# An int8-style decoder layer on one core: an earlier gamma/beta load, one joint scale chain for weights and activations, context products inside the QKV maximum pass, and bf16 diagonals

## The chip, the cores and the metric

The kernel runs on one core of one Trainium2 chip. The metric is the device time of one execution in microseconds (us). The kernel before took 493.25 us (median of 3 runs, 491.62 to 495.28). The profiled execution took 491.34 us, of which the trace covers a span of 489.4 us; the remaining 1.9 us lie around the span.

The engines are PE (TensorE), PEld (its weight load), DVE (VectorE), ACT (ScalarE), POOL (GpSimd) and SP (SyncE, which here only issues DMAs).

## The reference, cut to what matters

```python
def fq_floor(x):                    # fq_round is the same with round
    s = 2 ** ceil(log2(max(|x|) / 127))          # one scale for the WHOLE tensor
    return clip(floor(x / s), -128, 127) * s

h    = layernorm(x) * fq_round(ln_gamma) + fq_round(ln_beta)     # x: 8 x 256 x 128
qkv  = fq_floor(fq_floor(h) @ fq_round(w_qkv))                   # w_qkv: 128 x 3072
dots = fq_floor(q @ k.T * temp)                                  # 16 heads of 64, temp from exp(log_temp)
attn = fq_floor(softmax(dots))
out  = fq_floor(fq_floor(attn @ v) @ fq_round(w_out))
x    = layernorm(x + out)
# cross attention without softmax: q, k, v of 16 heads of 8 from x and the context (8 x 512 x 128);
# kv = sum over t of k[t] v[t], att = q @ kv * scale; x = layernorm(att + x), layernorm again outside
# MLP with affine quantisation and an exact gelu; x = layernorm(x + mlp)
```

Each `fq_` needs the maximum of a whole tensor before one element of it can be rounded. So the kernel computes the QKV product twice: once for its maximum (the maximum pass) and once for its codes (the code pass). It does the same with the dots.

Because the cross attention has no softmax, its context side folds into one 128 x 128 matrix for each batch. From the Gram matrix of the context, `gram = ctx^T [ctx | 1]`, come `a1 = gram Wv^T + bias`, then `kv`, then the matrix `xm`. These are the "context products".

## The kernel before, in words

The program is written out by hand for each engine, with semaphores between them. Each engine runs its list in order. Its stages on the time axis of the trace are these.

- **Prologue** (0 to 42.7 us). SP and ACT issue the loads. DVE takes the maximum of gamma and beta. The maximum goes across the partitions in `across_send` (the identity times the value of each partition, a 128 x 128 fp32 diagonal), a PE product with a matrix of ones (`across`), and `across_take` (a reduce of the result). `scale_of` makes the power of two and its inverse with three tiny DVE instructions. Then come the layernorm of x in 16 tiles of 128 tokens (`bn_stats`, `bn_aggr`, a square root on ACT, a Newton step, 16 instructions `norm`), PE transposes, gamma and beta applied while leaving PSUM (`hT`), and the maxima of `w_qkv` and of `hT` with a chain for each. Last come the integer codes of both (`h_codes`, `w_piece`), and on DVE the rounding of the temperature. ACT cannot start the maximum pass before DVE gets behind these seven tiny instructions, since DVE raises `qkv_folded` there.
- **QKV maximum pass** (42.7 to 78.9 us). It has 48 units of 128 x 1024, two matmuls each, in a ring of 4 slots of two PSUM banks, which are all 8 banks. Of every 4 units ACT takes the absolute value of 3 into bf16 (L835), and DVE folds each of those into a running maximum (L1164). DVE reads the fourth itself from PSUM (`absmax`, L1013). The loops over the four groups are hardware loops.
- **Between the passes**: DVE folds three running maxima into one and sends it across. PE makes the row sums of the context, both halves of `a1`, and in their midst the product with the diagonal. Then follows the **QKV code pass** (90.0 to 133.8 us), 48 units in a ring of 3 slots; banks 6 and 7 hold the other context products.
- Then the dots maximum pass, the dots code pass with the exponentials, the product with v, the output projection, the layernorms, the cross attention and the MLP.

In the trace, L476 is every matmul, L496 and L501 the PE transposes of the prologue, L1009 and L1010 every `tensor_scalar` of DVE, L1013 every maximum of absolute values, L1032 the reduce after `across`, L854 the codes on ACT. `mem` is the large SBUF array of which nearly every tile is a part, and `fold` is the store of the diagonals.

## Time and profile before

| | us |
|---|---|
| median of 3 runs | 493.25 (491.62 to 495.28) |
| profiled execution | 491.34 |
| its span | 489.4 |
| busy: DVE / ACT / PE / POOL | 423.3 / 341.4 / 240.0 / 153.3 |

The page cuts the span into 40 slices of 12.2 us and gives the busy share of each engine in tenths, and the clock granted to PE in tenths of 2.4 GHz. In a view in order of time a row reads: start, duration, engine, line, operation, tiles, and in brackets how long the engine was idle before it and what released it. A row with x2 or x16 holds that many merged instructions. An fp32 matmul appears as two records.

### The profile page before, as it was taken

The numbers are of one execution on the slowest core, as the hardware profiler recorded it, in microseconds if no ns is written. First come the engines' busy times: TensorE is split into PE (matmuls) and PEld (weight loads), VectorE is DVE, ScalarE is ACT, GpSimd is POOL, SyncE is SP. The second block draws the span as 40 slices with busy tenths as digits, with TensorE's granted clock in tenths as the row PEclk, the third lists the DMA queues.
The fourth block names the chain that finished last, engine by engine and source line by source line (L and its number), as shares of the span: only waits on it lengthen the run. The fifth ranks groups of instructions, "written<-read, shape, count | busy, mean of one in ns | idle before, by whom it ended". The sixth has DMA issues, their size and how long they took to land.

```text
span 489.4 us, 7119 instructions
## 1 busy us (share of the span) xinstructions
PE 240.0 (49%) x1538; PEld 108.3 (22%) x1546; DVE 423.3 (86%) x1415; ACT 341.4 (70%) x765; POOL 153.3 (31%) x324
## 2 busy tenths in 40 slices
PE   0096667988667763122222222207999528305031
PEld 0081123433212211011111111102333425202021
DVE  0898997497989998999999999969896986987967
ACT  1018993588899991999999999983677735636233
POOL 4700000200100000688888888881000003530010
PEclk9998996699955555555555555557999775557557
DMA  8500000000044432288888888876000400000002
GB/s 275 128 0 1 0 0 0 1 23 21 22 186 177 172 129 109 66 190 184 184 187 188 187 188 187 188 150 140 2 1 1 146 1 1 0 1 1 0 0 86
DMA packets 84207, 43.13 MB, mean 88 GB/s; under 512 B 69063, under 2 KB 74455, under 8 KB 84058
## 3 DMA queue, kind: packets, MB, share of 16 engines
q1 hardware_dynamic: 82090, 42.16, 33.2%
q10 hardware_dynamic: 2096, 0.73, 0.7%
q8 instruction: 8, 0.13, 0.1%
q14 instruction: 13, 0.11, 0.1%
HBM read 7.75 MB, written 1.58 MB: 19 GB/s over the span
## 4 chain that ended last, share of the span: by engine, by line
DVE 55%; PE 26%; issue 10%; ACT 5%; DMA 2%; DVEq 1%; ACTq 0%
PE ps L476 25%; DVE mem L1258 12%; DVE d_max L1013 8%; DVE mem L1010 6%; DVE mem L1449 2%; DVE row_max L1258 2%; DMA gbc<-in_L_attn_ln_beta 2%; DVE m L1586 2%; DVE m L1587 2%; DVE mem L1164 2%; DVE neg_max L1009 1%; ACT mem L888 1%; DVE r_now L1009 1%; ACT mem L854 1%; DVE row_code L1009 1%
## 5 line engine op out<-in xcount | busy, mean ns | idle before, releaser
L476 PE MATMUL ps<-mem 64*128 64x256 bf16 (+5 forms) x1181 | 176.0, 356 | 133.5 <-DMA mem<-mem 81.3
L888 ACT ACTIVATE mem<-mem,neg_max 128x256 f32<-128x256 int16 x256 | 126.3, 494 | 13.6 <-DVE neg_max L1009 9.7
L476 PEld LDWEIGHTS ps<-mem 64*128 64x128 bf16 (+4 forms) x1188 | 71.3, 122 | 234.4 <-issue 146.1
L1258 DVE CUSTOM_DVE_ANT_0 mem<-ps,fold,c 128x256 int16<-128x256 f32 x256 | 111.3, 471 | 0.0
L434 POOL TENSOR_SCALAR mem<-mem,r_now 128x256 int16<-128x256 f32 x176 | 80.9, 478 | 81.4 <-DVE r_now L1009 81.4
L1164 DVE TENSOR_TENSOR mem<-mem 128x1024 bf16<-128x1024 bf16 x84 | 54.4, 690 | 3.5 <-ACT mem L835 3.5
L835 ACT ACTIVATE mem<-ps,c 128x1024 bf16<-128x1024 f32 x48 | 48.3, 1291 | 1.6 <-PE ps L476 1.6
L888 ACT ACTIVATION_READ_ACCUMULATOR mem<-mem,neg_max 128x1 f32 x256 | 47.7, 186 | 0.0
L854 ACT ACTIVATE mem<-ps,c 128x1024 int16<-128x1024 f32 x32 | 36.3, 1210 | 13.9 <-PE ps L476 13.8
L434 POOL TENSOR_SCALAR bv_fine<-mem,r_now 128x256 int16<-128x256 f32 x80 | 36.8, 478 | 5.0 <-DVE r_now L1009 5.0
L1013 DVE TENSOR_REDUCE d_max<-ps 128x1024 f32 (+1 forms) x34 | 38.0, 1127 | 0.0
L1010 DVE TENSOR_SCALAR mem<-mem,c 128x2048 bf16<-128x2048 int16 (+2 forms) x44 | 34.7, 811 | 3.6 <-PE ps L476 3.4
L835 ACT ACTIVATE mem<-ps 128x1024 bf16<-128x1024 f32 x36 | 34.2, 1031 | 2.6 <-DVEq L1144 1.9
L476 PE MATMUL ps<-fold,ones 128*128 128x128 f32 (+2 forms) x18 | 7.3, 499 | 50.6 <-DVE fold L1009 50.6
L446 POOL TENSOR_TENSOR mem<-mem 128x512 f32<-128x512 f32 x4 | 5.0, 1267 | 77.3 <-ACT mem L945 77.3
L902 ACT ACTIVATE mem<-ps 128x1024 bf16<-128x1024 f32 x15 | 15.4, 1025 | 19.3 <-PE ps L476 19.3
L476 PE MATMUL ps<-minus,mem 128*128 128x256 bf16 x128 | 25.8, 285 | 2.5 <-DVE mem L1010 2.5
L1010 DVE TENSOR_SCALAR mem<-ps,c 128x1024 int16<-128x1024 f32 (+1 forms) x17 | 21.8, 1283 | 1.0 <-PE ps L476 0.9
L409 POOL MEMSET mem<- 128x3072 bf16 x1 | 2.7, 2657 | 62.5 <-DVE c L1009 62.5
L1258 DVE DVE_READ_ACCUMULATOR2_ANT row_max<- 128x1 f32 x256 | 20.1, 78 | 0.0
L1215 DVE CAST mem<-mem 128x1024 bf16<-128x1024 int16 x32 | 12.4, 422 | 6.7 <-ACT mem L854 6.7
L905 ACT ACTIVATE mem<-ps 128x1024 f32<-128x1024 f32 x16 | 16.4, 1022 | 2.5 <-DVE d_max L1013 2.5
(202 smaller groups left out, 371.5 us busy)
## 6 DMA issues: line engine op xcount, KB each, us to landing
mem<-mem SPq DMA_DIRECT2D x64, 256.0 KB, 2.4
mem<-in_L_attn_w_qkv SPq DMA_DIRECT2D x1, 1536.0 KB, 9.4
mem<-in_x SPq DMA_DIRECT2D x1, 1024.0 KB, 5.5
out<-mem SPq DMA_DIRECT2D x4, 256.0 KB, 2.2
mem<-in_x ACTq DMA_DIRECT2D x1, 512.0 KB, 5.5
mem<-in_x SPq DMA_DIRECT2D x1, 512.0 KB, 4.8
xattn_matrix<-mem SPq DMA_DIRECT2D x1, 512.0 KB
mem<-in_L_attn_w_out SPq DMA_DIRECT2D x1, 512.0 KB, 5.0
```

Source lines behind the costliest of these rows:

```text
L434: ins = pl.tensor_scalar(fine_ring[slot][:, u, pos * N:(pos + 1) * N], e_ring[:, unit % 4, pos], r_now[:, unit % 4, pos:pos + 1], FLOOR, A ...
L476: return te.matmul(o_, l_, r_, start=start, stop=stop)
L835: sc.activation(abs_t[:, k % 3], ps[:, s:s + 2].rearrange("p a n -> p (a n)"), ACT.Abs, scale=scale).then_inc(sem(f"{phase}_max_act"), 1)
L854: sc.activation(code_i[:, k % 4], ps[:, s:s + 2].rearrange("p a n -> p (a n)"), ACT.Identity, scale=col("g_qkv"), bias=col("floor")).then_ ...
L888: ins = sc.activation(e_ring[:, u % 4, pos], y_ring[:, u % 4, pos], ACT.Exp, scale=scale_reg, bias=neg_max[:, u % 4, pos:pos + 1], accum_o ...
L902: sc.activation(abs_o[nth % 4], src, ACT.Abs, scale=GROW).then_inc(sem("o_abs"), 1)
L905: sc.activation(o_pair(nth // 4, nth % 4), src, ACT.Copy).then_inc(sem("o_read"), 1)
L1009: return ve.tensor_scalar(o_, i_, s1, None, op0)
L1010: return ve.tensor_scalar(o_, i_, s1, s2, op0, op1)
L1013: return ve.tensor_reduce(o_, i_, AX.X, ALU.max, apply_absolute_value=True)
L1164: ve.tensor_tensor(run_max[:, k % 3], run_max[:, k % 3], abs_t[:, k % 3], ALU.max)\
L1258: ins = ve.tensor_tensor_reduce(y_ring[:, slot, pos], ps[:, 2 * slot + pos // 2, (pos % 2) * N:(pos % 2 + 1) * N], shift, col("g_dots"), - ...
```

## The change

- **Loads.** Both halves of x are issued by SP, in front of `w_qkv` and the context. ACT's queue begins with gamma and beta; the second half of x no longer stands ahead of them.
- **Prologue on DVE.** The statistics of the first eight tiles of x stand between sending and taking gamma's and beta's maximum. Half of the 16 `norm` go to ACT, which gets a shift `nmr0` for them. Both halves of `hT` are made on ACT. The maxima of `w_qkv` and `hT` go through one chain (`wh_scale`). The growth factor is in the diagonal instead of an instruction of its own. The temperature is computed behind the scale of QKV.
- **POOL.** The two products that spread the biases (`bv_sel`, `bk_sel`) become 16 ACT instructions on 8 partitions ahead of the square root. The temperature's chain on POOL comes before the memset of `run_max`, which now waits for gamma's codes.
- **Maximum pass.** It is written out without loops and has a ring of 3 slots. Banks 6 and 7 hold the context products, which PE does between units: half of a batch's Gram matrix after each of the units 6 to 21, the sums after 27, `a1` after 28, 31, 32 and 34. ACT takes them out after units 13, 20, 24, 28 and 37. DVE's last fold is done after the others have been joined (in both maximum passes).
- **After it.** PE makes the first three units of the code pass before the product with the diagonal. That product is bf16 for QKV, dots and the attention output (`across_bf`).

```diff
@@ sync, pool @@
-            sp.dma_start(x_in_pairs[:, halves[0]], x_pairs[:, halves[0]]).then_inc(sem("x_first"), 16)
+            for half in range(2):
+                batches = slice(half * B // 2, (half + 1) * B // 2)
+                sp.dma_start(x_in_pairs[:, batches], x_pairs[:, batches]).then_inc(sem(f"x_half{half}"), 16)
...
-            pl.memset(run_max, 0.0).then_inc(sem("run_max_zero"), 1)
-
-            eye = ident[0:B, 0:B].rearrange("p (b o) -> p b o", o=1).to_broadcast((B, B, D))
-            pool.wait_ge(sem("bkv_loaded"), 32)
-            pl.tensor_tensor(bv_sel, bkv[:, 1:2].to_broadcast((B, B, D)), eye, ALU.mult)
-            pl.tensor_tensor(bk_sel[:], bkv[:, 0:1].to_broadcast((B, B, D)), eye, ALU.mult)\
-                .then_inc(sem("bias_rows"), 1)
...
+            pool.wait_ge(sem("gb_codes"), 1)
+            pl.memset(run_max, 0.0).then_inc(sem("run_max_zero"), 1)
@@ tensor @@
+            def across_bf(bank):
+
+                n_across[0] += 1
+                pe.wait_ge(sem("diagonals"), n_across[0])
+                mm(ps[:, bank, 0:P], ones_bf[:], diag_b[:, 0]).then_inc(sem("across"), 1)
...
+            def gram_half(b, part):
+                bank, pos = (6, 7, 6)[b // 3], b % 3
+                for k in range(2 * part, 2 * part + 2):
                     last = mm(ps[:, bank, pos * (D + 1):(pos + 1) * (D + 1)], ctx_sb[:, 4 * b + k, 0:D],
                               ctx_sb[:, 4 * b + k], k == 0, k == 3)
...
+            def ctx_work(n):
...
+                if n == 18:
+                    pe.wait_ge(sem("gram_ready"), 1)
+                if 6 <= n < 22:
+                    gram_half((n - 6) // 2, n % 2)
+                if n == 27:
+                    pe.wait_ge(sem("gram_ready"), 3)
+                    pe.wait_ge(sem("bias_rows"), 1)
+                    sums_of_ctx()
+                if n == 28:
+                    a1_main(0)
+                if n == 31:
+                    pe.wait_ge(sem("cs_r2"), 1)
+                    a1_bias(0)
+                if n == 32:
+                    a1_main(1)
+                if n == 34:
+                    a1_bias(1)
...
-            with pe.Fori(0, GROUPS) as gi:
+            for gi in range(GROUPS):
                 for u in range(QKV_UNITS):
...
                     qkv_unit(gi, u, u % QKV_MAX_RING).then_inc(sem("qkv_max_unit"), 1)
...
+                    ctx_work(gi * QKV_UNITS + u)
...
-            a1_half(0)
             pe.sem_inc(sem("dots_max_unit"), 2 * STAGES)
-
-            across(5, diag, 1)
-            a1_half(1)
...
                     qkv_unit(gi, u, u % QKV_RING).then_inc(sem("qkv_code_unit"), 1)
+                    if n == QKV_RING - 1:
+                        across_bf(7)
@@ scalar @@
-            act.dma_start(x_in.rearrange("p (b c) d -> p b (c d)", c=2)[:, B // 2:B],
-                          x.rearrange("b (p c) d -> p b (c d)", c=2)[:, B // 2:B]).then_inc(sem("x_second"), 16)
             act.dma_start(gbc[:, 0:1], at_g[:, None]).then_inc(sem("gb_loaded"), 16)
...
+            for b in range(B):
+                sc.activation(bv_sel[:, b], bkv[:, 1], ACT.Copy, scale=ident[0:B, b:b + 1])
+                ins = sc.activation(bk_sel[:, b], bkv[:, 0], ACT.Copy, scale=ident[0:B, b:b + 1])
+            ins.then_inc(sem("bias_rows"), 1)
             sqrt_of("ln0")
+            act.wait_ge(sem("ln0_shift"), 1)
...
+                for part, at_n, bank, b0, nb in ((0, 13, 6, 0, 3), (1, 20, 7, 3, 3), (2, 24, 6, 6, 2)):
+                    if n == at_n:
                         act.wait_ge(sem("gram_ps"), part + 1)
@@ vector @@
+            def across_bf(bank):
+
+                ts(diag_b[:, 0], ident_b[:], col("m"), None, ALU.mult).then_inc(sem("diagonals"), 1)
+                across_take(1, bank, col("x"))
...
-            link(ts(x6[:, 0:2], x6[:, 0:2], GROW, None, ALU.mult))
             scale_of(x6[:, 0:2], 2, s4[:, 0:2], i4[:, 0:2])
...
+            across(m6[:, 2:4], 2, diag6[:, 2:4], 7, x6[:, 2:4], 2)
+            scale_of(x6[:, 2:4], 2, s4[:, 2:4], i4[:, 2:4], done="wh_scale")
```

The first place is DVE's list from the maximum of gamma and beta on. Before:

```order
L1013 TENSOR_REDUCE m<-gbc 128x2
L1009 TENSOR_SCALAR mem<-ident,m 128x128 x2
L1032 TENSOR_REDUCE x<-ps 128x2
L1009 TENSOR_SCALAR x<-x 128x2
L1010 TENSOR_SCALAR s<-x 128x2
L1009 TENSOR_SCALAR s<-s 128x2
L1010 TENSOR_SCALAR i<-s 128x2
L1009 TENSOR_SCALAR gb_i<-gbc,i 128x1 x2
L1009 TENSOR_SCALAR c<-gb_i,s 128x1 x2
L1067 BN_STATS mem<-mem 128x6 x16
```

And now, with what each row waits for:

```order
L1058 TENSOR_REDUCE m<-gbc 128x2 [waits gb_loaded,consts]
L1055 TENSOR_SCALAR mem<-ident,m 128x128 [waits dve_chain]
L1113 BN_STATS mem<-mem 128x6 [waits x_half0]
L1113 BN_STATS mem<-mem 128x6 x7
L1082 TENSOR_REDUCE x<-ps 128x2 [waits across]
L1055 TENSOR_SCALAR s<-x 128x2 [waits dve_chain]
L1054 TENSOR_SCALAR s<-s 128x2 [waits dve_chain]
L1055 TENSOR_SCALAR i<-s 128x2 [waits dve_chain]
```

Eight statistics moved into the wait for PE, and the row `x<-x 128x2` is gone.

The second place is PE between the passes. Before:

```order
L566 MATMUL ps<-ident,mem 8x128 [waits qkv_max_dve,qkv_max_act,bias_rows]
L476 MATMUL ps<-xw_T,mem 8x128
L476 MATMUL ps<-bkv,s 8x128
L476 MATMUL ps<-xw_T,mem 128x128 x4
L476 MATMUL ps<-bv_fine,cs_T 128x512 [waits cs_T]
L476 MATMUL ps<-fold,ones 128x128 [waits diagonals]
L476 MATMUL ps<-bv_fine,cs_T 128x512
L476 MATMUL ps<-mem 128x512 [waits qkv_code_act]
```

And now:

```order
L475 MATMUL ps<-mem 128x512 [waits qkv_max_act]
L475 MATMUL ps<-mem 128x512 [waits qkv_max_dve]
L475 MATMUL ps<-mem 128x512
L475 MATMUL ps<-diag_b,ones_bf 128x128 [waits diagonals]
L475 MATMUL ps<-mem 128x512 [waits qkv_code_act]
```

Only units of the code pass stand ahead of the product with the diagonal; the context products are further up, between units of the maximum pass.

## Rows read from the trace of the kernel before

**Rows 1.** The page, part 2: busy tenths and granted clock in 40 slices

```profile
DVE  0898997497989998999999999969896986987967
...
PEclk9998996699955555555555555557999775557557
```

**Rows 2.** DMA issues of the first 30 us: KB, us from issue to landing

```profile
mem<-in_x SPq DMA_DIRECT2D x1, 512.0 KB, 4.8
```

**Rows 3.** In order of time, 0 to 26 us

```profile
3.46 0.30 POOL L376 TENSOR_SCALAR ident_b<-ident 128x128 bf16<-128x128 f32 x1
...
11.88 0.15 DVE L1013 TENSOR_REDUCE m<-gbc 128x2 f32<-128x2 f32 x1 [11.88 <-DMA gbc<-in_L_attn_ln_beta]
...
13.93 0.42 DVE L1032 TENSOR_REDUCE x<-ps 128x2 f32<-128x256 f32 x1 [1.38 <-PE ps L476]
14.27 1.89 POOL L384 TENSOR_TENSOR bk_sel<-bkv,ident 8x1024 f32<-8x1024 f32 x1
14.39 1.79 DVE L1009 TENSOR_SCALAR x<-x 128x2 f32<-128x2 f32 x1
...
17.17 0.19 POOL L389 TENSOR_SCALAR c<-lt 128x1 f32<-128x1 f32 x1 [1.02 <-DMA lt<-in_L_attn_log_temp]
...
21.87 0.31 ACT L800 ACTIVATE sd<-mem,c 128x16 f32<-128x16 f32 x1 [13.82 <-DVE mem L1071]
...
23.82 0.19 POOL L405 TENSOR_TENSOR c<-c 128x1 f32<-128x1 f32 x1
```

**Rows 4.** In order of time, 25 to 46 us

```profile
27.62 1.34 DVE L1010 TENSOR_SCALAR mem<-ps,c 128x1024 f32<-128x1024 f32 x1
...
29.75 3.74 PE L476 MATMUL ps<-mem 128*128 128x129 f32 x32
...
35.28 0.28 DVE L1032 TENSOR_REDUCE x<-ps 128x1 f32<-128x128 f32 x1
...
36.42 0.28 DVE L1032 TENSOR_REDUCE c<-ps 128x1 f32<-128x128 f32 x1
...
40.83 0.43 DVE L1117 CAST mem<-mem 128x1024 bf16<-128x1024 int16 x1
...
42.67 3.77 ACT L835 ACTIVATE mem<-ps 128x1024 bf16<-128x1024 f32 x4 [1.88 <-DVEq L1144]
```

**Rows 5.** DVE's groups by shape, 0 to 136 us: count, busy us, mean ns, idle before

```profile
L1010 DVE TENSOR_SCALAR mem<-mem,rsd 128x128 f32<-128x128 f32 x16 | 4.2, 342 | 0.0
```

**Rows 6.** One group of 12 units of the maximum pass as a window: busy of PE, PEld, DVE, ACT, POOL; clock

```profile
48.30:57.10 8.80, 6.11 (x23) 1.77 (x24) 8.80 (x14) 8.62 (x10) 0.00 (x0) 1.00 0.00 0
```

**Rows 7.** ACT's groups by shape, 0 to 190 us

```profile
L858 ACT ACTIVATE mem<-ps 128x1024 f32<-128x1024 f32 x1 | 1.0, 1022 | 0.0
L819 ACT ACTIVATE mem<-ps 128x387 f32<-128x387 f32 x2 | 0.9, 478 | 0.0
...
L843 ACT ACTIVATE cs_T<-ps 8x128 f32<-8x128 f32 x1 | 0.3, 266 | 1.9 <-PE ps L566 1.9
```

**Rows 8.** In order of time, 74 to 112 us

```profile
80.48 2.08 PE L476 MATMUL ps<-xw_T,mem 128*128 128x128 f32 x8
82.48 2.07 PE L476 MATMUL ps<-bv_fine,cs_T 8*128 8x512 f32 x2
...
84.48 0.80 PE L476 MATMUL ps<-fold,ones 128*128 128x128 f32 x2
...
85.32 0.29 DVE L1032 TENSOR_REDUCE c<-ps 128x1 f32<-128x128 f32 x1 [2.18 <-PE ps L476]
...
86.54 2.66 POOL L409 MEMSET mem<- 128x3072 bf16 x1 [62.53 <-DVE c L1009]
...
89.32 4.11 PE L476 MATMUL ps<-mem 128*128 128x512 bf16 x9 [0.33 <-issue]
...
91.28 0.43 DVE L1215 CAST mem<-mem 128x1024 bf16<-128x1024 int16 x1 [4.49 <-ACT mem L854]
...
97.80 1.02 PE L476 MATMUL ps<-mem,xw_T 128*128 128x512 f32 x2
```

More of the change, by code:

```diff
@@ L491, in _ @@
             across(7, diag6, 2)
-            for half in range(2):
-                pe.wait_ge(sem("xn_ready"), half + 1)
-                for t in range(8 * half, 8 * half + 8):
+            for q in range(4):
+                pe.wait_ge(sem("xn_ready"), q + 1)
+                pe.wait_ge(sem("xn_act"), q + 1)
+                for t in range(4 * q, 4 * q + 4):
                     last = te.transpose(ps[:, t // 4, (t % 4) * P:(t % 4 + 1) * P], xn[:, t], ident[:])
-                last.then_inc(sem("xnT_ps"), 1)
+                if q % 2:
+                    last.then_inc(sem("xnT_ps"), 1)
             pe.wait_ge(sem("xw_loaded"), 48)
@@ L589, in kv_bias @@
                 for b in range(4 * half, 4 * half + 4):
-                    last = mm(ps[:, 6 + half, (b % 4) * P:(b % 4 + 1) * P], bk_sel[:, b], r2[:, 0],
+                    last = mm(ps[:, 6 + half, (b % 4) * P:(b % 4 + 1) * P], bk_sel[:, b], r2,
                               False, b % 4 == 3)
@@ L1081, in _ @@
             link(ve.tensor_tensor(rsd[:], rsd[:], newton[:], ALU.mult))
-            for t in range(TILES):
-                ins = norm(xn, x_in, t)
-                if t % 8 == 7:
-                    ins.then_inc(sem("xn_ready"), 1)
-            dve.wait_ge(sem("gb_codes"), 1)
-            dve.wait_ge(sem("xnT_ps"), 1)
-            ts(hT[:, 0:UNIT], ps[:, 0:2].rearrange("p a n -> p (a n)"), col("gamma"), col("beta"),
-               ALU.mult, ALU.add).then_inc(sem("hT_ready"), 1)
-            dve.wait_ge(sem("w_loaded"), 16)
@@ L1150, in max_pass @@
                     order.insert(u - EARLY, u)
-                with dve.Fori(0, iters) as i:
+                for i in range(iters):
                     for u in order:
@@ L1166, in max_pass @@
[L1166 to L1177 removed]
+                            continue
```

280 lines of the change are left out of this document (147 added, 133 removed).

## The prediction

> **What bounds the kernel now.** I read the page's slices first, then the prologue in order of time with its DMA issues, then one group of the maximum pass as a window, then the rows between the passes.
>
> The slices [rows 1] show DVE at nine tenths almost everywhere and at nothing in the first slice. So what shortens DVE's own list, or the time before that list begins, comes off the end. The second line shows PE's clock high (2.4 GHz) through slice 5, that is to 73 us, low (1.2 GHz) for a good part of slices 6 and 7, around the end of the maximum pass, and high again in the code pass. The change touches four places.
>
> - **The start.** DVE's first instruction comes at 11.88, released by beta's landing [rows 3]. The first half of x, at the head of SP's queue, landed 4.8 after its issue, near 5.6 [rows 2]. The constants were ready at 3.76 [rows 3]. The order of loads costs DVE some 7 us.
> - **The prologue** is one chain on DVE from 11.88 to ACT's first row of the maximum pass at 42.67, which was idle for 1.88 until DVE raised a semaphore [rows 4].
> - **The maximum pass.** In 8.80 us DVE is busy 8.80, ACT 8.62 and PE 6.11 [rows 6]. Two engines are full, and the third has 2.7 us to spare for every 12 units, 0.733 us for each unit.
> - **Between the passes** DVE waits 2.18 for PE and 4.49 for ACT [rows 8], while PE makes context products at the low clock.
>
> **The change, part by part.**
>
> *Loads, -6.9.* Beta would now be issued near 1.4, with no half of x ahead on its queue. Its landing isn't in the trace. The floor is 3.8, where the constants are ready; the ceiling is 11.9, if nothing improves. The nearest row is x's first half, at 5.6, with a thousand times the bytes. I take 5.0: 11.9 - 5.0 = 6.9.
>
> *DVE's chain to the first maximum unit, -7.4.*
> - PE's first product: DVE waited 1.38 [rows 3]. Eight statistics fill that: -1.4.
> - The growth instruction `x<-x`: -1.8 [rows 3], see below.
> - Eight of 16 `norm` go to ACT. Sixteen are busy 4.2 [rows 5]: -2.1.
> - The half of `hT` that DVE made: -1.3 [rows 4]. ACT makes it under DVE's maximum of `w_qkv`, which doesn't need it.
> - The temperature lies between the last cast, ending at 41.26, and 42.67 [rows 4]: -1.4. It comes back below.
> - The joint chain saves the stretch from one reduce to the other (35.28 to 36.42 [rows 4]), 1.1, but its double-width product makes DVE wait 1.38 as the first did, and the second diagonal and wider reduce add about 0.1: +0.4. The shift `nmr0` is another small instruction, +0.2 as an estimate.
>
> The 16 ACT copies that replace POOL's products take at most 0.27 each, 4.3 in all [rows 7]. They stand ahead of the square root. That came at 21.87, 10.0 after DVE's first instruction [rows 3]. Now it is due 10.0 - 1.4 - 1.8 = 6.8 after it, near 11.8. If the biases land by 7.5 the copies are hidden and cost nothing. If they land where they did (POOL's first product ended when its second began, at 14.27), the square root is late; that belongs to the first rival.
>
> *The memset of `run_max` and DVE, +1.3.* The 1.79 of `x<-x` at 14.39 end at 16.18. POOL's product with `bk_sel` ran from 14.27 to 16.16 [rows 3]. A DVE instruction of two elements per partition stood still until POOL had finished. The change removes this pair, but moves POOL's 2.66 memset [rows 8]. It used to run while DVE had nothing to do. Now it follows the temperature's chain on POOL, which ran from 17.17 to 24.01 [rows 3]; it may begin up to 3 us sooner, since the loads ahead of `lt` move up. So the memset lies somewhere from 21 to 27. By the sums above, DVE is then at the joint diagonals, the scale chain or the first codes, all SBUF to SBUF `tensor_scalar`. The old memset shows nothing, since DVE then had only one-element instructions. Bounds: 0 and 2.66; I take the middle, 1.3. The Trainium skill, page "SBUF — State Buffer", section "Who interferes with whom", speaks against the change here: a VectorE instruction in a two-port mode (`tensor_scalar` and casts can be) and any GpSimd instruction exclude each other for the whole instruction, writes included. The pair at 14.27 agrees with it. By that rule the term is near 2.7 instead of 1.3, and the sum 1.4 higher.
>
> *Context products in the maximum pass, +4.8.* A unit costs PE 6.11/12 = 0.51, perhaps 0.47 without gaps. Gram: 32 records in 3.74 [rows 4] are 16 matmuls, so a half of two matmuls is 0.47. Units 6 to 21 then cost PE 0.94 to 0.98 against a cadence of 0.733: 16 x 0.2 to 0.25 = 3.3 to 3.9 too much. A ring of three slots lets PE be about two units ahead at the start, worth 1.5: +2.2. The halves of `a1` took 2.08 and 2.07 at 1.2 GHz [rows 8]; at 2.4 GHz I take 1.04 and 1.02 (the 512-column product at 97.80 [rows 8]), twice 2.06, and 0.8 for the sums: 4.9 in units 27 to 34. Eight units leave PE 8 x 0.733 - 8 x 0.49 = 2.0. The remaining 2.9, less the same cushion, is +1.4. ACT's outputs of Gram (0.48 each [rows 7]) fall where PE is late anyway. That of `a1`, 1.02 [rows 7], falls behind it, where ACT is full: +1.0. The smaller ring adds perhaps 0.2. Bounds: +2.0, if PE keeps up and only ACT's outputs count; +7.8, with no cushion (3.9 + 2.9 + 1.0).
>
> *Between the passes, -5.1.* DVE's 2.18 for PE hold the `a1` product ahead of the diagonal and 0.80 of fp32 [rows 8]. One bf16 pass is one record instead of two: 0.4. With half of a diagonal's write, -1.9. The 4.49 for ACT's first code go, because three units stand ready. The temperature takes 1.3 of that place: -3.2. The fold's new order saves nothing: the same instructions still follow DVE's own last maximum.
>
> *Code pass, -1.0:* ACT's output of `a1` is gone. Bounds 0, if DVE is full regardless, and -2, with PE warm sooner.
>
> *The rest, -1.4:* bf16 diagonals for dots and output, 0.5 each as above; two growth instructions, 0.2 each as an estimate. Loops written out on DVE: nothing, the loop shows no gap at DVE 8.80 of 8.80.
>
> Sum: -6.9 - 7.4 + 1.3 + 4.8 - 5.1 - 1.0 - 1.4 = **-15.7**. The profiled execution of 491.34 becomes 475.6. The median shown is 1.9 higher, so I say **477.5**.
>
> **The rivals.**
>
> - *Beta or the biases stay late (12%).* For it: tiny loads took 9.9 where x took 4.8, and their packets share the DMA engines with x's. Against: they no longer follow half of x. The first term vanishes: 477.5 + 6.9 = 484.4.
> - *The full lock (13%).* The page's rule taken as a mechanism of this kernel: a diagonal or the first code of `hT` waits for the memset's end, 2.66. 478.9.
> - *The context products are free (12%).* PE's 2.7 spare per group times four is 10.8, and the products need 16 x 0.47 + 4.9 = 12.4; if matmuls overlap better than records show, only ACT's 2.0 stay: 474.7, and with the copies well hidden 473.
> - *Slower: PE falls to 1.2 GHz in the maximum pass (5%).* The clock fell near the end of the pass [rows 1] and stayed low from 80 to 89 although PE had fp32 products one after another: 0.80 for one across, 2.07 for 512 columns against 1.02 later [rows 8]. Now PE idles before the pass, then half of its work is fp32. At the low clock nine records of a unit take 4.11 [rows 8], 0.91 per unit, 44 for 48; Gram doubles to 15, the rest to 10: 69 against about 36 now, +33 in place of +4.8. That gives 505.7. It is slower than before as soon as about 60% of the pass runs low. Against: Gram ran at full speed after fp32 transposes [rows 4], and a bf16 unit now follows every piece.
>
> The forecast has 55%; 3% are left for what I don't see. Its own range is 472 to 482.5.
>
> **Range and chances.** Down: the pass at +2.0 (-2.8), no lock (-1.3), beta at 3.8 (-1.2), code pass -2 (-1.0), not all at once: 470.5. Up: the pass at +7.8 (+3.0), full lock (+1.4), copies partly open (+1.5) is 483.4; the late beta is 484.4, so 484.5. A measurement here tells about 1% from no change, 488.3 to 498.2. Only the clock case lies above it, 5%; 3% for within; 92% faster.
>
> **What would show it.** DVE's first row near 5 and statistics behind it; ACT's first row of the maximum pass near 29 to 30; that pass near 41 long, with DVE and ACT idle on PE in units 6 to 21 and 28 to 35; ACT's first code without a wait for PE; a DVE `tensor_scalar` that ends with the memset. Wrong if beta lands after 8, if the clock row shows 5 in slices 2 to 5, or if the pass lasts 36 or 46.

## The result and the profile after

The changed kernel takes **480.39 us** (median of 4 runs, 479.80 to 482.28), the kernel before beside it on the same chip 492.47. The ratio is 0.976, 95% interval 0.973 to 0.979. Its profiled execution took 479.80, with a span of 478.0, against 491.34 and 489.4 before. The forecast was 477.5, its range 470.5 to 484.5.

Since nearly every row moved, the two traces are compared at landmarks that both have. Times are from the start of the span; "pass" is the QKV maximum pass.

| stretch | before | after | difference | forecast |
|---|---|---|---|---|
| start to DVE's reduce of gamma and beta | 11.88 | 5.46 | -6.42 | -6.9 |
| to ACT's first absolute value of the pass | 30.79 | 25.20 | -5.59 | -6.1 (-7.4 and +1.3) |
| to the end of DVE's last maximum of the pass | 36.20 | 41.33 | +5.13 | +4.8 |
| to ACT's first code | 11.17 | 7.38 | -3.79 | -5.1 |
| DVE's first cast to the dots' first absolute value | 42.99 | 42.81 | -0.18 | -1.0 |
| all that follows, and what lies between these | | | -0.55 | -1.4 |
| span | 489.4 | 478.0 | -11.4 | -15.7 |

The page's slices of the changed kernel, DVE's busy tenths and PE's granted clock, answer to [rows 1]:

```profile
DVE  5879897889899999999999999958986985977967
...
PEclk9969995999755555555555555558999775557557
```

DVE works in the first slice. The clock is now low in parts of slices 2 and 6 (from 24 and from 72 us), in both of which PE had stopped. Before, it was low from 77.5 to 94.6 us, although PE was busy for 15.5 of the 17 us from 78 to 95. Both kernels thus open the code pass at the low clock, and that turns out to matter.

**The prologue**, in order of time, answers to [rows 3]:

```profile
5.46 0.15 DVE L1058 TENSOR_REDUCE m<-gbc 128x2 f32<-128x2 f32 x1 [5.46 <-DMA gbc<-in_L_attn_ln_beta]
...
8.68 0.40 ACT L823 ACTIVATE bv_fine<-bkv,ident 8x128 f32<-8x128 f32 x1 [0.71 <-DMA bkv<-in_L_xattn_bv]
...
13.36 0.29 ACT L816 ACTIVATE sd<-mem,c 128x16 f32<-128x16 f32 x1
13.69 0.25 DVE L1133 RECIPROCAL rsd<-sd 128x16 f32<-128x16 f32 x1 [1.49 <-ACT sd L816]
...
21.99 2.66 POOL L404 MEMSET mem<- 128x3072 bf16 x1
...
22.84 1.96 DVE L1055 TENSOR_SCALAR mem<-ident,m 128x128 f32<-128x128 f32 x2
24.85 1.22 PE L475 MATMUL ps<-mem,ones 128*128 128x256 f32 x2 [5.25 <-DVE mem L1055]
26.11 0.42 DVE L1082 TENSOR_REDUCE x<-ps 128x2 f32<-128x256 f32 x1 [1.31 <-PE ps L475]
```

Two things are to be seen. The square root stands at 13.36 directly behind the 16 copies, and DVE waits 1.49 for it: the copies are not hidden. And the two diagonals at 22.84, of a form that took 0.48 for two at 5.65, take 1.96 and end at 24.80, just behind the memset's end at 24.65.

**The pass.** PE in a window over units 6 to 21 (columns as in [rows 6]), and ACT's rows in the same stretch and at the output of `a1`:

```profile
36.00:47.70 11.70, 11.70 (x84) 9.66 (x83) 10.81 (x14) 9.48 (x12) 0.00 (x0) 1.00 0.01 2
```

```profile
36.92 2.85 ACT L873 ACTIVATE mem<-ps 128x1024 bf16<-128x1024 f32 x3 [0.65 <-PE ps L475]
...
40.42 1.94 ACT L873 ACTIVATE mem<-ps 128x1024 bf16<-128x1024 f32 x2 [0.65 <-PE ps L475]
...
63.41 1.03 ACT L860 ACTIVATE mem<-ps 128x1024 f32<-128x1024 f32 x1
```

PE is busy 11.70 of 11.70 where it was busy 6.11 of 8.80 [rows 6], and ACT waits for it once in every four units, which now take 3.50 (36.92 to 40.42) instead of 2.93. The granted clock is 1.00 there.

**Between the passes**, answering to [rows 8]:

```profile
76.28 0.29 PE L475 MATMUL ps<-diag_b,ones_bf 128*128 128x128 bf16 x1 [3.63 <-DVE diag_b L1054]
76.60 0.29 DVE L1082 TENSOR_REDUCE c<-ps 128x1 f32<-128x128 f32 x1 [0.38 <-PE ps L475]
...
79.37 4.63 ACT L903 ACTIVATE mem<-ps,c 128x1024 int16<-128x1024 f32 x4 [8.51 <-DVEq L1250]
80.61 0.43 DVE L1265 CAST mem<-mem 128x1024 bf16<-128x1024 int16 x1 [1.32 <-ACT mem L903]
...
84.66 1.28 DVE L1055 TENSOR_SCALAR mem<-ps,c 128x1024 int16<-128x1024 f32 x1 [1.29 <-PE ps L475]
...
85.09 1.20 ACT L903 ACTIVATE mem<-ps,c 128x1024 int16<-128x1024 f32 x1 [1.09 <-PE ps L475]
```

DVE waits 0.38 for PE instead of 2.18. But ACT's first code is released by DVE's sequencer: a semaphore that DVE raises behind the temperature. And 4 us into the code pass both engines wait for PE, at the low clock.

### The profile page after: what moved, and what is told of

It is laid out like the page before. It is cut to its first block, busy times and chain, and to the rows that moved or that the text cites. A ratio compares the mean times of both kernels' runs of the same rounds, so it can differ in the third digit from the quotient of the medians.

```text
span 478.0 us, 6808 instructions
## 1 busy us (share of the span) xinstructions
PE 233.2 (49%) x1541; PEld 106.5 (22%) x1541; DVE 420.0 (88%) x1396; ACT 350.2 (73%) x789; POOL 149.9 (31%) x323
## 4 chain that ended last, share of the span: by engine, by line
DVE 53%; PE 21%; issue 16%; ACT 7%; DMA 1%; DVEq 1%; ACTq 0%
PE ps L475 20%; DVE mem L1308 12%; DVE mem L1055 6%; DVE mem L1213 4%; DVE d_max L1058 4%; DVE mem L1496 2%; DVE row_max L1308 2%; DVE m L1633 2%; DVE m L1634 2%; ACT mem L903 2%; ACT mem L933 1%; DVE r_now L1054 1%; DMA bkv<-in_L_xattn_bv 1%; DVE row_code L1054 1%; DVE neg_max L1054 1%
## 5 line engine op out<-in xcount | busy, mean ns | idle before, releaser
L475 PEld LDWEIGHTS ps<-mem 64*128 64x128 bf16 (+3 forms) x1188 | 72.2, 122 | 229.0 <-issue 126.7
L1058 DVE TENSOR_REDUCE d_max<-ps 128x1 f32<-128x1024 f32 (+1 forms) x34 | 38.0, 1126 | 0.3 <-PE ps L475 0.3
L1055 DVE TENSOR_SCALAR mem<-mem,c 128x2048 bf16<-128x2048 int16 (+2 forms) x42 | 33.3, 814 | 3.8 <-PE ps L475 3.7
L475 PE MATMUL ps<-fold,ones 128*128 128x128 f32 (+2 forms) x10 | 4.6, 559 | 44.3 <-DVE fold L1055 44.3
L1055 DVE TENSOR_SCALAR mem<-ps,c 128x1024 int16<-128x1024 f32 x16 | 20.5, 1281 | 1.5 <-PE ps L475 1.5
L971 ACT ACTIVATE sd<-mem,c 128x4 f32<-128x4 f32 x16 | 4.6, 295 | 18.5 <-DVE mem L1503 18.3
```

The lines of the kernel that those rows point to most:

```text
L475: return te.matmul(o_, l_, r_, start=start, stop=stop)
L1055: return ve.tensor_scalar(o_, i_, s1, s2, op0, op1)
L1058: return ve.tensor_reduce(o_, i_, AX.X, ALU.max, apply_absolute_value=True)
```

## The experiments

All kernels are compared by the same landmarks, since gains of a microsecond drown in the total. "Beta" is DVE's first row, the others are the lengths of the stretches of the table above; beta, stretches and span come from one profiled execution. The last two columns are the ratio to the kernel before and its interval, over all executions.

| kernel | beta | to the pass | pass | to code | code pass | span | ratio | 95% |
|---|---|---|---|---|---|---|---|---|
| before | 11.88 | 30.79 | 36.20 | 11.17 | 42.99 | 489.4 | | |
| changed | 5.46 | 25.20 | 41.33 | 7.38 | 42.81 | 478.0 | 0.976 | 0.973-0.979 |
| changed, again | 7.46 | 23.77 | 41.32 | 7.37 | 42.79 | 478.5 | 0.977 | 0.974-0.980 |
| e1 temperature late | 7.76 | 23.52 | 41.32 | 6.18 | 43.91 | 478.7 | 0.974 | 0.971-0.977 |
| e2 copies late | 6.74 | 23.95 | 41.32 | 7.38 | 43.23 | 478.5 | 0.977 | 0.975-0.980 |
| e3 memset early | 7.44 | 22.46 | 41.32 | 7.38 | 43.95 | 478.6 | 0.973 | 0.970-0.976 |
| e4 half the Gram | 7.04 | 24.22 | 39.18 | 7.38 | 43.91 | 477.8 | 0.971 | 0.968-0.973 |
| e5 PE kept busy | 6.83 | 24.18 | 41.31 | 7.33 | 42.02 | 477.6 | 0.970 | 0.967-0.974 |
| e6 products respread | 7.16 | 25.09 | 37.70 | 7.45 | 44.25 | 477.8 | 0.970 | 0.967-0.974 |
| e7 a1 output late | 7.42 | 23.57 | 40.66 | 7.45 | 44.33 | 479.8 | 0.976 | 0.971-0.981 |
| o1 before, new loads | 7.33 | 31.17 | 36.19 | 11.17 | 43.11 | 485.3 | 0.987 | 0.984-0.990 |
| o2 before, ring of 3 | 11.98 | 32.34 | 36.48 | 10.14 | 42.59 | 490.5 | 1.000 | 0.998-1.002 |
| c1 all | 3.94 | 27.81 | 37.48 | 6.13 | 42.22 | 473.7 | 0.965 | 0.961-0.969 |
| c2 all, Gram split | 3.94 | 22.76 | 37.53 | 6.12 | 42.02 | 469.1 | 0.959 | 0.956-0.962 |

### The temperature behind the semaphore

```diff
-            temperature()
...
             dve.sem_inc(sem("cast_a"), 4)
+            temperature()
```

> Only the temperature's seven DVE instructions move, from ahead of the two semaphore increments that free ACT's code slots to behind them. Theory A (ACT's first code waits for those increments, not for the scale): ACT's first code comes 0.3 us after the scale instead of 1.7, and DVE's first cast about 1.3 us sooner against the scale; whole kernel 1.0 to 1.3 faster than the changed kernel (480.4), near 479.2. Theory B (the first code waits for PE or for the scale itself, the temperature is covered): the gap from scale to first code stays at 1.7 and the time at 480.4.

Measured: 479.94 us (479.28 to 480.76). ACT's first code comes 6.18 behind DVE's last maximum instead of 7.38:

```profile
78.78 2.30 ACT L903 ACTIVATE mem<-ps,c 128x1024 int16<-128x1024 f32 x2 [7.31 <-DVEq L1249]
```

The term is real, 1.20. But the code pass took 43.91 instead of 42.81, and 1.1 of the gain was gone in this execution. The move has a side effect too: DVE's first wide cast of the code pass now meets POOL's second memset and takes 1.36, where it took 0.43 at 80.61.

```profile
78.44 2.66 POOL L408 MEMSET mem<- 128x3072 bf16 x1 [53.18 <-DVE c L1054]
80.01 1.36 DVE L1265 CAST mem<-mem 128x1024 bf16<-128x1024 int16 x1
```

This is a rival for the lost 1.1, but the other runs speak against it. In e3 and e4 the cast takes 0.43 and the code pass is as long (43.95, 43.91). In c2 it takes 1.36 and the pass is 42.02, as in e5, where it takes 0.43.

### The copies behind xw_T

```diff
-            act.wait_ge(sem("bkv_loaded"), 32)
-            for b in range(B):
-                sc.activation(bv_sel[:, b], bkv[:, 1], ACT.Copy, scale=ident[0:B, b:b + 1])
-                ins = sc.activation(bk_sel[:, b], bkv[:, 0], ACT.Copy, scale=ident[0:B, b:b + 1])
-            ins.then_inc(sem("bias_rows"), 1)
             sqrt_of("ln0")
...
             sc.activation(xw_T[:].rearrange("p k n -> p (k n)"), ps[:, 6, 0:2 * P], ACT.Copy).then_inc(sem("xw_T"), 1)
+            act.wait_ge(sem("bkv_loaded"), 32)
...
```

> The 16 bias copies on ACT move from ahead of the first square root to behind the copy of the cross-attention weights, where ACT idles about 6 us. Theory A (the copies made the square root late): the square root starts near 12.1 instead of 13.36, DVE's wait of 1.49 for it goes down to about 0.3, and everything behind moves up by 1.2; near 479.2. Theory B (the square root is bound by DVE's statistics): the square root stays where it is. If the memset on POOL keeps its place in time while DVE's diagonals come 1.2 sooner, part of the gain shows up as a longer or shorter stall there: the diagonals would then meet the memset at its very start, so up to 1.2 may be lost again.

Measured: 481.28 us (480.29 to 481.33), no gain. DVE's wait for the square root is gone,

```profile
13.64 0.25 DVE L1133 RECIPROCAL rsd<-sd 128x16 f32<-128x16 f32 x1 [0.17 <-ACT sd L816]
```

but it comes at 13.64, where it came at 13.69. Beta had landed at 6.74 instead of 5.46. In the changed kernel's second profile (beta at 7.46, copies in front) the same row waits 0.17 as well. So DVE's chain and ACT's copies end nearly together at the square root: the copies cost 1.3 only when beta lands early. They take away what an early landing would give.

### The memset in front of the temperature's chain on POOL

```diff
+            pool.wait_ge(sem("gb_codes"), 1)
+            pl.memset(run_max, 0.0).then_inc(sem("run_max_zero"), 1)
             pool.wait_ge(sem("lt_loaded"), 16)
...
-            pool.wait_ge(sem("gb_codes"), 1)
-            pl.memset(run_max, 0.0).then_inc(sem("run_max_zero"), 1)
```

> POOL's memset of the running maxima moves ahead of the temperature's chain, so that it runs right after gamma's codes, from about 9.4 to 12.0, under DVE's statistics. Theory A (the memset held DVE's SBUF to SBUF tensor_scalar): the two diagonals at 22.8 take 0.48 together instead of 1.96, and all behind moves up by 1.5; near 478.9. DVE's bn_stats and bn_aggr are not slowed. Theory B (the long diagonal has another cause, such as the reduce before it): it stays at 1.96 and the time at 480.4.

Measured: 479.41 us (478.49 to 480.50). The diagonals take 0.48 again:

```profile
23.54 0.48 DVE L1055 TENSOR_SCALAR mem<-ident,m 128x128 f32<-128x128 f32 x2
24.07 0.50 PEld L475 LDWEIGHTS ps<-mem,ones 128*128 128x128 f32 x2 [3.85 <-DVE mem L1055]
24.07 1.22 PE L475 MATMUL ps<-mem,ones 128*128 128x256 f32 x2 [3.61 <-DVE mem L1055]
```

From beta to the pass it is 22.46, against 23.77 in the second profile of the changed kernel, which had beta at the same time: 1.3 for the lock. Again the code pass was longer, 43.95.

### Half of the Gram matrix left out

```diff
-                for k in range(2 * part, 2 * part + 2):
+                for k in range(2 * part, 2 * part + 1):
...
-                              ctx_sb[:, 4 * b + k], k == 0, k == 3)
+                              ctx_sb[:, 4 * b + k], k == 0, k == 2)
```

> Leaves out half of the Gram matmuls (one of the two in each piece), so the context products of units 6 to 21 cost PE 0.23 instead of 0.47 us each. Theory A (PE bounds units 6 to 21, 0.875 us for each where 0.735 would do): the pass falls from 41.3 us by 16 x 0.14 = 2.2 or a little more, to 39; near 478.1. Theory B (the ring of 3 slots sets the pace there, not PE's work): the pass stays above 40.5. Theory C (ACT's extra evictions alone lengthen the pass): it stays at 41.3.

Measured: 478.25 us (477.87 to 479.50). The pass is 39.18, 2.14 shorter, so PE's Gram work is the binding load in units 6 to 21. The code pass of the profiled execution gave back 1.1 for the third time.

### PE kept busy between the passes

```diff
                     if n == QKV_RING - 1:
+                        for k in range(16):
+                            mm(ps[:, 6, :], w5[:, 0, 0, 0], hT_codes[:, 0:BANK])
                         across_bf(7)
+                        for k in range(18):
+                            mm(ps[:, 6, :], w5[:, 0, 0, 0], hT_codes[:, 0:BANK])
```

> The changed kernel with 16 and 18 products more on PE around the bf16 product with the diagonal, into bank 6, whose values nobody reads; nothing else is changed. In the changed kernel PE stands idle from 72.65 to 80.63 but for 0.29 us, its granted clock falls to 0.50 at about 74, and comes back to 1.00 only at 83.8, and the code pass opens with DVE waiting 1.29 and 0.20 for PE and ACT 1.09 and 0.42. In the four experiments before, every gain ahead of the code pass was given back in part there: from DVE's first cast to the dots' first absolute value 42.81 us in the changed kernel, 43.91, 43.23, 43.95 and 43.91 in those. Theory A (the low clock at the start of the code pass eats what is won ahead of it): the clock stays at 1.00 from 72 on, the waits of 1.29 and 1.09 go, the stretch takes 41.2 to 41.7, and the time falls to about 478.7 (ratio to the kernel before 0.972). Rival B (the code pass is bound by DVE and ACT all through, the waits only move): the stretch stays at 42.8 to 43.9 and the time at 480 to 481. Rival C (the added products themselves delay PE's next units): the time rises by 0.5 to 1.

Measured: 479.16 us (478.91 to 479.81). The granted clock reads 1.00 in every window from 64 to 88 us, where it was 0.50 from 74 to 83. The rows that answer to the two waits of the code pass, 1.29 and 1.09 in the changed kernel:

```profile
83.94 1.28 DVE L1059 TENSOR_SCALAR mem<-ps,c 128x1024 int16<-128x1024 f32 x1 [0.43 <-PE ps L475]
...
84.37 1.20 ACT L907 ACTIVATE mem<-ps,c 128x1024 int16<-128x1024 f32 x1 [0.23 <-PE ps L475]
```

The code pass takes 42.02: 0.8 less than in the changed kernel, and 1.9 less than in e1, e3 and e4. The expectation, 41.2 to 41.7, was a little too low. What PE adds here is work that nobody needs.

The granted clock in windows of 1 us goes with the spread. Except in e5, c1 and c2 it stands at 0.50 when PE takes up the code pass and rises to 1.00 some time later:

| kernel | PE restarts | clock high again | between | code pass |
|---|---|---|---|---|
| e5, c2, c1 | | always high | | 42.02, 42.02, 42.22 |
| changed | 80.63 | 83.8 | 3.1 | 42.81 |
| changed, again | 81.18 | 84.3 | 3.1 | 42.79 |
| e2 | 80.64 | 84.5 | 3.8 | 43.23 |
| e1 | 80.04 | 85.0 | 4.9 | 43.91 |
| e4 | 79.08 | 84.0 | 5.0 | 43.91 |
| e3 | 79.86 | 84.9 | 5.0 | 43.95 |
| e6 | 78.66 | 84.4 | 5.7 | 44.25 |
| e7 | 80.36 | 86.3 | 5.9 | 44.33 |

(The rise is worked out from the window whose mean lies between 0.50 and 1.00.) In these kernels the code pass grows with the time that PE runs it at the low clock, in one order without exception. The rise does not move with the restart. e2 restarts where the changed kernel does and is raised 0.7 later. So in a single execution a gain of one microsecond ahead of this point arrives at the end as something between nothing and all of it. With PE kept at work the pass took 42.0 to 42.2 each time.

Each row is one execution, and those of e1, e3 and e4 were among the longer ones of their kernels: 0.5, 0.9 and 1.25 above the medians. The medians themselves are 0.45, 0.98 and 2.14 below the changed kernel's 480.39 (on another chip its median was 481.25, so they are good to about a microsecond). Over several executions more of the gains arrives than these profiles show, and that of e4 about in full.

### The context products respread

```diff
-                bank, pos = (6, 7, 6)[b // 3], b % 3
+                bank, pos = (4, 5, 6)[b // 3], b % 3
...
+            for b in range(B):
+                if b == 6:
+                    pe.wait_ge(sem("xw_T"), 1)
+                for part in range(2):
+                    gram_half(b, part)
+            across(7, diag6[:, 2:4], 2)
...
-                if 6 <= n < 22:
-                    gram_half((n - 6) // 2, n % 2)
...
+                if 9 <= n < 13:
+                    a1_main(n - 9)
...
+                if 20 <= n < 24:
+                    a1_main(n - 16)
```

The sums stand after unit 6 and the biases of `a1` after 16 and 27. ACT takes the Gram matrix out ahead of the codes of `w_qkv`, and `a1` behind its last unit.

> The changed kernel with the context products in other places: the whole Gram matrix in PE's idle time of the prologue (19.6 to 24.85), in banks 4 to 6, taken out by ACT there, where it is idle from 20.9 to 27.2; the sums and the eight a1 products one by one after units 6 to 27; the output of a1 on ACT behind its last unit of the maximum pass. Theory A (what the pass grew by is PE's Gram and a1 work beside units of 0.49 at a cadence of 0.733, plus ACT's outputs): the pass, 41.33 long from ACT's first absolute value to the end of DVE's last maximum, falls to 35.5 to 36.5, as before the change or shorter; PE's clock doesn't fall at 23, so that the joint product with the diagonals takes 0.6 instead of 1.22 and DVE waits 0.7 instead of 1.31. Half a microsecond to one is given back at the start of the code pass, where PE's clock is low. The time falls by 5 to about 475.4 (ratio 0.965). Rival B (the Gram matrix waits for the context, which lands at 20.0 to 20.5, and delays the joint product): up to 1 us of it is lost, 476.4. Rival C (the pass is slower for its ring of three slots, not for PE's load): the pass stays at 38 or more, and the time above 477.

Measured: 479.55 us (478.63 to 479.69), far less than expected. The pass fell by 3.6, to 37.70, still 1.2 above the upper end of what was expected; no run isolates what remains. But above all the Gram matrix stood in front of the joint product:

```profile
19.91 7.31 PE L475 MATMUL ps<-mem 128*128 128x129 f32 x64
27.06 0.60 PE L475 MATMUL ps<-mem,ones 128*128 128x256 f32 x2
```

```profile
27.70 0.42 DVE L1080 TENSOR_REDUCE x<-ps 128x2 f32<-128x256 f32 x1 [2.66 <-PE ps L475]
```

It has 64 records, where the row in [rows 4] that the expectation went by holds 32, and takes 7.31 against 5.25 of idle time. The joint product itself took 0.60 instead of 1.22: PE had not stopped, and its clock was 1.00 there, where it was 0.50. The code pass gave back another 1.4, to 44.25.

### The output of a1 late

```diff
-                if n == 37:
-                    act.wait_ge(sem("a1_ps"), 2)
...
             qkv_max_units()
+            act.wait_ge(sem("a1_ps"), 2)
+            sc.activation(a1.rearrange("p b d -> p (b d)"), ps[:, 6:8].rearrange("p a n -> p (a n)"),
+                          ACT.Copy).then_inc(sem("a1_ready"), 1)
...
+                        pe.wait_ge(sem("a1_ready"), 1)
                         across_bf(7)
```

> The changed kernel with ACT's output of a1 (1.03 us at 63.41) moved behind ACT's last unit of the maximum pass, where ACT is idle from 71 to 79; PE waits for it ahead of the bf16 product with the diagonal. Theory A (the output stands in full in the pass, as the prediction had it, +1.0): the pass, 41.33 long in the changed kernel, takes 40.2 to 40.5, and the time falls by up to 1, with some of it given back in the code pass. Rival B (PE was late there anyway, by its a1 products, and ACT would only have waited for it): the pass stays within 0.3 of 41.33.

Measured: 481.41 us (480.10 to 481.78). The pass is 40.66, so the output cost 0.67 there, not 1.03. The whole gain went to the code pass, the longest of all. What follows it was 0.6 longer as well, and why stays open.

### The loads alone, on the kernel before

```diff
+            sp.dma_start(x_in_pairs[:, halves[1]], x_pairs[:, halves[1]]).then_inc(sem("x_second"), 16)
...
-            act.dma_start(x_in.rearrange("p (b c) d -> p b (c d)", c=2)[:, B // 2:B],
-                          x.rearrange("b (p c) d -> p b (c d)", c=2)[:, B // 2:B]).then_inc(sem("x_second"), 16)
             act.dma_start(gbc[:, 0:1], at_g[:, None]).then_inc(sem("gb_loaded"), 16)
```

> The kernel before with the new order of loads alone: the second half of x on SP's queue, gamma and beta at the head of ACT's. Gamma and beta landed at 5.46, 7.76, 6.74, 7.44 and 7.04 in the five profiled runs of the new order, at 11.88 in the kernel before. Theory A (DVE's list simply starts earlier): DVE's first row comes at 5.5 to 7.8, the landmarks behind it move by as much, and the time falls by 4 to 6.4, to 487.5 (ratio 0.990). Rival B (what comes behind, the second half of x or POOL's products with the biases and its temperature, holds DVE up): the landmarks at the first unit of the maximum pass move by less than 3, and the time is above 489.5.

Measured: 487.52 us (487.29 to 487.56). DVE starts 4.55 sooner, and 4.1 of the span's 489.4 are gone. The trace shows something else as well, the lock in its old place:

```profile
8.45 1.89 POOL L384 TENSOR_TENSOR bv_fine<-bkv,ident 8x1024 f32<-8x1024 f32 x1 [2.04 <-DMA bkv<-in_L_xattn_bv]
10.31 1.89 POOL L385 TENSOR_TENSOR bk_sel<-bkv,ident 8x1024 f32<-8x1024 f32 x1
```

```profile
9.84 0.53 DVE L1008 TENSOR_SCALAR x<-x 128x2 f32<-128x2 f32 x1
10.40 1.82 DVE L1009 TENSOR_SCALAR s<-x 128x2 f32<-128x2 f32 x1
```

`x<-x` ends at 10.37 with POOL's first product, and now it is the next instruction, `s<-x`, that takes 1.82 and ends at 12.22 with the second. In the kernel before, `x<-x` took 1.79 [rows 3]. So that 1.8 was the price of POOL's products. Had only the growth instruction been dropped, the next one would probably have been held in its place (no run tests that alone); taking the products off POOL removes both.

### A ring of three slots, on the kernel before

```diff
-        QKV_MAX_RING = 4
+        QKV_MAX_RING = 3
```

> The kernel before with a ring of three slots instead of four in the maximum pass, and nothing else. Theory A (with PE busy 6.11 of 8.80 in a group, three slots are enough): the pass, 36.20 from ACT's first absolute value to the end of DVE's last maximum, grows by 0.0 to 0.4, and the time stays at 492 to 494, ratio 0.998 to 1.002. Rival B (the smaller ring is a good part of the 5.1 us by which the pass grew): the pass grows by 1 to 3, and the time by as much.

Measured: 492.58 us (490.90 to 493.94), ratio 1.000. The pass is 36.48 instead of 36.20: +0.28. The total says less, since two other stretches moved. In this execution POOL's products began at 12.00 instead of 12.34 and so met DVE's two diagonals, which took 3.66 instead of 0.48:

```profile
12.00 1.88 POOL L383 TENSOR_TENSOR bv_fine<-bkv,ident 8x1024 f32<-8x1024 f32 x1 [5.59 <-DMA bkv<-in_L_xattn_bv]
12.17 3.66 DVE L1009 TENSOR_SCALAR mem<-ident,m 128x128 f32<-128x128 f32 x2
13.86 1.88 POOL L384 TENSOR_TENSOR bk_sel<-bkv,ident 8x1024 f32<-8x1024 f32 x1
```

They end together with POOL's second product, and `x<-x` behind them takes 0.17. That is the 1.55 by which the stretch to the pass is longer in the table. Between the passes 1.03 came back, as PE's clock stayed high until 82.5 there, where it fell at 77.5.

### The changed kernel again

> The changed kernel once more, beside c2 on the same chip, since gamma's and beta's landing moved from 5.46 to 7.76 us between profiled runs. Theory A (the landing at 5.46 was an early one): gamma and beta land at 6.7 to 7.8, the copies on ACT then delay the square root by under 0.3 us, and the first unit still comes at 30.7 to 31.3, as ACT's copies set the square root in either case. The time is 479 to 481, ratio 0.974. Rival B (the landing is at 5.5 as a rule): the square root waits 1.3 for the copies again.

Measured: 481.25 us (480.18 to 482.56). Beta landed at 7.46, and the pass began at 31.23 instead of 30.66. In the ten profiled runs that have both loads at the head of ACT's queue it landed at 6.74 to 7.76 nine times, and once at 5.46.

### All of it, and then with the Gram matrix split

```diff
+            sp.dma_start(gbc[:, 1:2], at_b[:, None]).then_inc(sem("gb_loaded"), 16)
             for half in range(2):
                 batches = slice(half * B // 2, (half + 1) * B // 2)
```

With it go the edits of e1, e3, e5 (14 and 13 products) and e6; the eight copies for `bv` stand behind `xw_T`, those for `bk` behind the output of `a1`.

> The changed kernel with all that the experiments point to: beta's load at the head of SP's queue, gamma's at the head of ACT's; the memset of run_max ahead of the temperature on POOL; the eight copies for bv behind xw_T and the eight for bk between the passes; the context products as in the run e6; the temperature behind the semaphore that ACT's first code waits for; 14 and 13 products more on PE around the product with the diagonal, to keep its clock up. Theory A (each is its own term): against the changed kernel, memset and joint product -2.1, beta -1.5, pass -5.3, temperature -1.2, start of the code pass -1.5: 480.4 - 11 = about 469.5, range 468 to 472 (ratio to the kernel before 0.953). Rival B (gains ahead of the code pass are given back in it): 472 to 475.

Measured: 476.19 us (474.91 to 477.33). The temperature's gain came (6.13) and the code pass kept it (42.22). The pass took 37.48, 1.4 more than expected. The largest miss, against an expected 469.5, is the term of e6 again, larger, since DVE now came sooner:

```profile
27.20 0.42 DVE L1087 TENSOR_REDUCE x<-ps 128x2 f32<-128x256 f32 x1 [5.70 <-PE ps L476]
```

Then the Gram matrix was split, with two batches ahead of the joint product, three behind it and three in the pass:

```diff
+            for b in range(2):
+                for part in range(2):
+                    gram_half(b, part)
             across(7, diag6[:, 2:4], 2)
+            pe.wait_ge(sem("xw_T"), 1)
+            for b in range(2, 5):
+                for part in range(2):
+                    gram_half(b, part)
...
+                if n in (4, 6, 8, 10, 12, 14):
+                    gram_half(5 + (n - 4) // 4, n // 2 % 2)
```

> The run c1 with the Gram matrix split differently. In e6 and c1 its 64 records took 7.31 and 6.98 us in one piece, longer than PE's idle time in the prologue, and the joint product waited behind them: DVE waited 2.66 and 5.70 for it. Now only batches 0 and 1 (1.8 us) stand ahead of the joint product, batches 2 to 4 (2.7) in PE's wait behind it (2.8 long), and the halves of 5 to 7 after the units 4 to 14; sums after unit 20, the a1 products after 21 to 35. Theory A (the joint product needs PE free at about 21.4, and the terms of c1 hold otherwise): ACT's first absolute value of the maximum pass comes at 26.5 to 27.5 instead of 31.75, the pass takes 36.5 to 37.5, the stretch from DVE's first cast to the dots' first absolute value 42.0 to 42.5, and the time is 4.5 to 5 below c1: about 471.5, ratio 0.955. Rival B (something else then holds the first unit, such as the copies on ACT or the landing of the context): the first unit comes at 28 to 30 and the time is 473 to 475.

Measured: **472.02 us** (470.88 to 473.25), ratio 0.959 to the kernel before, where the changed kernel had 0.977 in the same comparison. 472.02 over its 481.25 is 0.981. About 471.5 had been expected.

```profile
21.50 0.60 PE L476 MATMUL ps<-mem,ones 128*128 128x256 f32 x2
...
22.14 0.43 DVE L1096 TENSOR_REDUCE x<-ps 128x2 f32<-128x256 f32 x1 [1.29 <-PE ps L476]
...
26.70 4.69 ACT L881 ACTIVATE mem<-ps 128x1024 bf16<-128x1024 f32 x5 [0.26 <-PE ps L476]
```

The pass begins at 26.70, 5.05 sooner than in c1. The clock line of its page stays at eight tenths or more through the first ten slices:

```profile
PEclk9999999998555555555555555559999767557556
```

## Why the prediction was right, and where it was off

The direction held, and so did most of the mechanisms and about three quarters of the size. The sum said -15.7 and the spans moved by -11.4. The 4.3 that are missing have their places, and beta's early landing at 5.46, which was luck, hides little of it, since the copies took most of it back. One sum of the range is off: the four terms downward add up to 6.3, which gives 471.2 even all at once, and not 470.5.

- **Loads, -6.9: measured -6.42, as a rule -4.4.** That they follow the queue's order was right (o1). The value of 5.0 was too early; ten profiles show 5.46 once and 6.74 to 7.76 nine times. The bound from x's first half at 5.6 was about the floor of what came, not its middle.
- **DVE's chain, -7.4, and the memset, +1.3: together -5.59, or -7.0 where beta was late.** The step that failed is that the copies are hidden. They began at 8.68, when their data had landed, not by 7.5, and the last began at 13.07 against a square root due at 12.2. Beta's landing and the copies make up for each other: both profiles of the changed kernel start the pass within 0.6 us.
- **The lock, +1.3:** measured 1.48 in the changed kernel's rows (1.96 less 0.48) and 1.3 by e3. It is the full lock of the rival; DVE reached its diagonals 0.85 after the memset began, so 1.81 of the 2.66 were left, of which it lost 1.48, and the term came out near the middle. The Trainium skill, "SBUF — State Buffer", section "Who interferes with whom", says that such a pair blocks for a whole instruction, for writes too: a memset reads nothing, and the rows agree. The row at 10.40 in o1 agrees as well.
- **`x<-x`, -1.8:** right in sum, and for the second of the two reasons that the prediction gives (o1). The size holds for the one execution that it was read from. In o1 POOL's products cost DVE 2.0, and in o2, which has the prologue of the kernel before, 3.2, by where they began.
- **Context products, +4.8: measured +5.13.** Gram, forecast 2.2, costs at least the 2.14 that half of it gives back (e4). The output of `a1` costs 0.67 instead of 1.0 (e7), the ring 0.28 instead of 0.2 (o2). 2.0 remain for the `a1` products, the sums and the Gram outputs, forecast at 1.4; no run isolated them, and the parts need not add up. Neither rival held: the products are not free, and the clock read 1.00 from 34 to 72 us. The load, not the ring, is the greater cause: spread as in e6 and c2, with three slots, the pass takes 37.5 to 37.7. That is still 1.0 to 1.2 more than in o2.
- **Between the passes, -5.1: measured -3.79.** This is the largest single miss. The prediction put the temperature "in that place", into DVE's wait for ACT. The program has it ahead of the semaphore for ACT's first code, so ACT waits for it too. With it behind (e1) the stretch is 6.18 and the difference -4.99, as forecast.
- **Code pass, -1.0: measured -0.18.** ACT's output of `a1` is gone from it (1.02 at 92.24 in the kernel before), but ACT spends the time waiting for PE: 1.09 at 85.09, where it had waited 0.50 at 95.95.

```profile
92.24 1.02 ACT L858 ACTIVATE mem<-ps 128x1024 f32<-128x1024 f32 x1
...
95.95 1.20 ACT L854 ACTIVATE mem<-ps,c 128x1024 int16<-128x1024 f32 x1 [0.50 <-PE ps L476]
```

The window in which the clock rose (columns as in [rows 6]; the mean clock is 0.71, so the rise lies near 94.6):

```profile
94.00:95.00 1.00, 1.00 (x3) 0.25 (x2) 0.43 (x1) 1.00 (x2) 0.00 (x0) 0.71 0.00 0
```

The step that failed is the silent one that PE would keep up there. The low clock is not new: it lasted until 94.6 in the kernel before and until 83.8 in the changed one, 3.3 and 3.2 us behind DVE's first cast. The prediction used "PE warm sooner" only for a lower bound. With PE kept at work the stretch is 42.02, which is the -1.0, but part of that would have come in the kernel before as well: in o2, whose clock rose 0.55 behind the first cast, the stretch took 42.59.
- **The rest, -1.4: measured -0.55 to the end.** The bf16 product gave 0.51 at the dots (the wait 0.89 became 0.38), as forecast, and 0.36 at the output (0.68 became 0.32). The last stretch, with the second product of the MLP, was 0.28 longer. It is the clock once more:

```profile
474.01 5.09 PE L476 MATMUL ps<-w2T,mem 128*128 128x128 bf16 x64 [7.27 <-DVE mem L1010]
...
477.43 0.75 DVE L1604 SCALAR_TENSOR_TENSOR mem<-ps,c,mem 128x512 f32<-128x512 f32 x1 [0.66 <-PE ps L476]
```

```profile
462.32 5.52 PE L475 MATMUL ps<-w2T,mem 128*128 128x128 bf16 x64 [7.27 <-DVE mem L1055]
...
466.03 0.75 DVE L1651 SCALAR_TENSOR_TENSOR mem<-ps,c,mem 128x512 f32<-128x512 f32 x1 [0.95 <-PE ps L475]
```

PE takes up these products at the low clock after an idle time of 7.27 in both kernels. Before, the clock rose 2.9 us later, after the change 3.7. In all fourteen profiles this stretch takes 22.60 where the rise came after 2.9, 22.69 after 3.1 (o1), and 22.87 to 22.89 where it came after 3.6 to 4.6.

## What to carry to other kernels

Compare an experiment at landmarks, not by the total of one execution: three edits that gained 1.2 to 2.1 us in their own stretch (e1, e3, e4) have spans within 0.7 of the changed kernel's, because a load landed later and a later stretch took 1.1 back. Their medians over four executions show more of the gain. Work moved into another engine's "idle" time is priced against that engine's spare time in the very units where it lands, and against what follows the idle time on its queue. Before calling a wait filled, look for the semaphore that stands behind the work in the program, since it may release somebody else.
